# Routed experts after a convolution block: tiles in pairs, weights in the gated product, one reduction per token tile

## The chip, the core and the metric

The kernel runs on one core of a Trainium2 chip. The metric is the device time in microseconds of one execution. TensorE (PE) multiplies, VectorE (DVE), ScalarE (ACT) and GpSimd (POOL) do elementwise work, SyncE (SP) issues most loads; GpSimd also issues the indirect scatters.

## The reference, cut to what matters

```python
u = x @ W_in + b_in                       # x: 8 batches x 512 tokens x 256
x0, x1, v = split(short_conv(u), 3)
v = causal_fft_conv(v * x1, filter, filter_bias)
x = layernorm(x + (v * x0) @ W_out + b_out)
probs = softmax(x @ gate_w.T)             # 16 experts, the best 4 of each token
combine = top-4 weights, normalised
act = silu(x @ w1[e].T) * (x @ w3[e].T)   # hidden size 128, for each chosen expert e
moe = sum over e of combine[e] * (act @ w2[e].T)
shared = silu(x @ sw1.T) * (x @ sw3.T) @ sw2.T
out = layernorm(x + moe + shared)
```

## The kernel before, in words

The program has three parts, each written by hand for each engine, with semaphores between the engines.

The first is a loop over the eight batches (`batches`, with a `body` for each engine). It makes the convolution of batch i+1 and the routing of batch i-1 in one body. For each token the routing finds the four experts, their weights (`m8` times `rden`) and a row number in a DRAM table `expert_rows`, sorted by expert. ScalarE copies each token's row four times into `row` (`fill_rows`), VectorE writes the weight and the later destination into two more columns (`end_rows`), and GpSimd issues 16 indirect scatters of 128 rows per batch (`scatter`). GpSimd also adds the output bias into `xtok` (its line is 611), which VectorE needs for the residual sum `r`. The shared expert's result, with the residual, goes into DRAM as the fifth part of each token (`store_acc`).

The second part runs the expert tiles (`tiles`, with a `turn` for each engine). A tile is 128 rows of one expert; there are 160, in 20 groups of eight: groups 0 to 13 hold batches 0 to 5, groups 14 to 19 batches 6 and 7. One turn works on four tiles at different stages: it transposes tile u, makes the hidden product of tile u-2 (`AT_H`), transposes the gated product `ta` of tile u-3 (`AT_A`), and multiplies tile u-4 by w2 (`AT_Y`). Every matrix is split into a high and a low half (`xtT_hi`, `xtT_lo`, `taT_hi`, `taT_lo`), so that three matmuls make one product. SyncE loads rows into `xt`, eight buffers; a buffer is free when VectorE has copied its last two columns into `wd` (semaphore `t_wd`). ScalarE scales the result by the weight into one of four `ty` buffers, and GpSimd scatters it into `token_parts`, where each token has five parts of 256 values side by side. A `ty` buffer is free when its scatter has landed (`res_out`). At the head of each group TensorE loads the expert numbers into registers. Groups 2 to 9 also carry the last batch's 16 row scatters, two in each.

The third part (`last`) sums the parts and normalises. SyncE loads the five parts of 128 tokens into a `yb` buffer, of which there are two sets of four. VectorE adds parts 0 and 1 into `s1` (line 1454), GpSimd makes parts 2, 3 and 4 into `s2` (lines 664 and 668), VectorE adds the two (line 1465) and takes statistics (line 1149); for the last token tile VectorE also adds the fifth part itself. In names of the trace `s1` is `r` or `acc`, and the `yb` buffers are `row`, `late_parts` and `more_parts`. Batches 0 to 4 are summed between the turns of groups 15 to 19, batches 5 to 7 in a tail behind them. While tiles run, VectorE finds the root of the variance by Newton steps (`norm_part`); in the tail ScalarE's root is used.

## Time and profile before

| what | value |
| --- | --- |
| median of three runs | 682.38 us (680.13 to 684.12) |
| the profiled execution | 681.89 us, its span 680.2 us |
| mean granted TensorE clock | 0.933 |
| busy: PE, DVE, ACT, POOL | 562.6, 531.9, 400.1, 430.9 us |
| traffic | 127.69 MB by DMA, mean 188 GB/s |
| expert tiles, first transpose to last product | about 366 to 645 us |

The span goes from the first to the last instruction of the profiled execution. Busy time is the union of an engine's instructions, so two that overlap count once. No engine is busy for the whole span; which one sets the pace changes from part to part, so the page's totals have to be read by stage.

### The profile page before, as it was taken

Reading aid. Unit: us, or ns where it says so; the run is one execution under the profiler, and the core shown is the slowest. Engines: PE = TensorE matmul, PEld = TensorE weight load, DVE = VectorE, ACT = ScalarE, POOL = GpSimd, SP = SyncE. Lnnn points to the kernel's source line nnn. Section 1 sums busy time; section 2 is a strip of 40 time slices with the busy share of each in tenths; the row PEclk is TensorE's granted clock in tenths of the full one; section 3 lists DMA queues with packets and bytes.
Section 4 is the critical chain, followed back from the end, with each engine's and each line's share of the span. In section 5 each row is a group of like instructions: output and inputs, shape, how many; then the busy total and the mean of one; then the engine's idle time right before and its main releaser. Section 6 shows DMA issues by size and latency. Waiting matters only on the chain.

```text
span 680.2 us, 13537 instructions
## 1 busy us (share of the span) xinstructions
PE 562.6 (83%) x3356; PEld 491.8 (72%) x3357; DVE 531.9 (78%) x1494; ACT 400.1 (59%) x968; POOL 430.9 (63%) x414
## 2 busy tenths in 40 slices
PE   1879798999999999997877999899999996777600
PEld 0558686888878877776666999898898985767500
DVE  5247889898989999999886766665666568899877
ACT  0443454776767585663162976776777774656632
POOL 2061325277767868585637677777776678778892
PEclk9769899999999999998968999999999999888955
DMA  8329812233424243219863778766665579988674
GB/s 306 97 66 365 310 35 63 82 129 93 140 86 156 93 139 108 93 62 347 274 179 125 206 218 234 229 197 184 186 186 177 163 267 356 292 287 285 237 301 155
DMA packets 77116, 127.69 MB, mean 188 GB/s; under 512 B 10870, under 2 KB 57527, under 8 KB 76474
## 3 DMA queue, kind: packets, MB, share of 16 engines
q1 hardware_dynamic: 45548, 69.34, 33.3%
q0 software_dynamic: 22448, 49.17, 21.3%
q10 hardware_dynamic: 9086, 8.80, 3.8%
q8 instruction: 12, 0.20, 0.1%
q14 instruction: 22, 0.18, 0.1%
HBM read 81.00 MB, written 54.72 MB: 200 GB/s over the span
## 4 chain that ended last, share of the span: by engine, by line
PE 41%; DVE 31%; issue 13%; DMA 5%; POOL 5%; ACT 4%; DVEq 1%; SPq 0%; POOLq 0%; ACTq 0%
PE bank L855 6%; PE bank L857 5%; PE bank L856 5%; PE bank L686 4%; PE bank L705 4%; PE bank L894 3%; POOL expert_rows L634 3%; DMA token_parts<-ty_all,wd 3%; PE bank L728 2%; PE bank L886 2%; PE bank L795 2%; DVE prodA L1209 2%; PE bank L816 2%; DVE x1c L1130 2%; POOL token_parts L647 2%
## 5 line engine op out<-in xcount | busy, mean ns | idle before, releaser
L647 POOL DMA_INDIRECT token_parts<-ty_all,wd x160 | 157.3, 983 | 63.3 <-issue 41.9
L634 POOL DMA_INDIRECT expert_rows<-row,slot x128 | 136.1, 1063 | 90.5 <-DVE dest L1367 53.6
L855 PE MATMUL bank<-w_hi,xtT_hi 128*128 x320 | 94.1, 294 | 20.3 <-issue 13.3
L1068 ACT ACTIVATE ty_all<-bank,wd 128x256 f32<-128x256 f32 x160 | 76.8, 480 | 36.2 <-DMA token_parts<-ty_all,wd 32.3
L1413 DVE TENSOR_TENSOR ta<-bank,tsl 128x128 f32<-128x128 f32 x160 | 46.3, 289 | 60.5 <-ACT tsl L1050 57.6
L856 PE MATMUL bank<-w_lo,xtT_hi 128*128 x320 | 91.3, 285 | 0.0
L857 PE MATMUL bank<-w_hi,xtT_lo 128*128 x320 | 91.0, 285 | 0.0
L855 PEld LDWEIGHTS bank<-w_hi,xtT_hi 128*128 128x128 f32 x320 | 61.9, 194 | 24.6 <-issue 24.6
L1426 DVE TENSOR_TENSOR xtT_lo<-bank,xtT_hi 128x256 fp32r<-128x256 f32 x160 | 67.6, 422 | 1.8 <-ACT xtT_hi L1061 1.6
L1050 ACT ACTIVATE tsl<-bank 128x128 f32<-128x128 f32 x160 | 44.4, 277 | 38.2 <-PE bank L857 35.0
L1061 ACT CAST xtT_hi<-bank 128x256 fp32r<-128x256 f32 x160 | 61.9, 387 | 6.9 <-PE bank L894 6.6
L894 PE MATMUL bank<-ident,xt 128*128 128x128 f32 x320 | 62.4, 278 | 2.7 <-issue 2.0
L857 PEld LDWEIGHTS bank<-w_hi,xtT_lo 128*128 128x128 f32 x320 | 62.0, 194 | 0.0
L856 PEld LDWEIGHTS bank<-w_lo,xtT_hi 128*128 128x128 f32 x320 | 61.8, 193 | 0.0
L855 PE MATMUL bank<-w_hi,taT_hi 128*128 x160 | 59.2, 370 | 0.4 <-DVE taT_lo L1419 0.3
L686 PE MATMUL bank<-zt,mats 128*128 128x256 f32 x256 | 57.6, 381 | 1.7 <-DVE slot L1322 1.7
L886 PE MATMUL bank<-ident,ta 128*128 128x128 f32 x160 | 46.0, 287 | 15.0 <-DVE ta L1413 14.8
L795 PE MATMUL bank<-mats,Y 128*128 128x256 f32 x256 | 58.0, 386 | 0.0
L686 PEld LDWEIGHTS bank<-zt,mats 128*128 128x128 f32 x256 | 47.9, 190 | 9.0 <-DVE slot L1322 2.8
L795 PEld LDWEIGHTS bank<-mats,Y 128*128 128x128 f32 x256 | 49.2, 194 | 6.7
L1055 ACT CAST taT_hi<-bank 128x128 fp32r<-128x128 f32 x160 | 42.5, 266 | 10.7 <-PE bank L886 10.6
L950 ACT ACTIVATE up<-bank,chan 128x512 f32<-128x512 f32 x48 | 33.1, 689 | 26.7 <-PE bank L705 26.5
(174 smaller groups left out, 1497.4 us busy)
## 6 DMA issues: line engine op xcount, KB each, us to landing
xt<-expert_rows SPq DMA_DIRECT2D x160, 129.0 KB
row<-token_parts SPq DMA_DIRECT2D x12, 640.0 KB, 5.2
more_parts<-token_parts SPq DMA_DIRECT2D x12, 640.0 KB, 8.1
late_parts<-token_parts SPq DMA_DIRECT2D x8, 640.0 KB, 7.4
expert_rows<-in_c_pad SPq DMA_DIRECT2D x2, 2064.0 KB, 13.2
expert_rows<-in_c_pad SPq DMA_DIRECT2D x32, 129.0 KB
xT_hi<-in_xT POOLq DMA_DIRECT2D x8, 512.0 KB, 4.5
xT<-in_xT SPq DMA_DIRECT2D x8, 512.0 KB, 3.8
```

The source lines that it names most:

```text
L634: pool.indirect_dma_start(out=rows_d, out_offset=bass.IndirectOffsetOnAxis(ap=slot[q][:, n:n + 1], axis=0), in_=row[:, n // TOPK, n % TOPK ...
L647: pool.indirect_dma_start(out=parts_d, out_offset=bass.IndirectOffsetOnAxis(ap=wd[:, v, 1:2].bitcast(U32), axis=0), in_=ty[v % 4], in_offs ...
L686: mm = te_.matmul(ps[:, part * D:(part + 1) * D], fwd[:, 2 * s + t, part * NF * P + f * P:part * NF * P + (f + 1) * P], src[:, 2 * s + t, ...
L795: mm = te_.matmul(bank[4 + c][:, s * 2 * P:(s + 1) * 2 * P], Y[:, f, s, part * D + c * P:part * D + (c + 1) * P], inv[:, part * NF + f, s ...
L855: te_.matmul(ps, x_hi, w_hi, start=first, stop=False)
L856: te_.matmul(ps, x_hi, w_lo, start=False, stop=False)
L857: return te_.matmul(ps, x_lo, w_hi, start=False, stop=last)
L886: te_.transpose(bank[4 + v % 2][:, 0:P], ta[:, v % 2, :], ident[:, :]).then_inc(t_aT, 1)
L894: mm = te_.transpose(bank[v % 2][:, c * P:(c + 1) * P], xt[:, v, c * P:(c + 1) * P], ident[:, :])
L1061: sc.copy(xtT_hi[:, v % 2, :, :].rearrange("p c t -> p (c t)"), bank[v % 2][:, 0:D]).then_inc(t_xhi, 1)
L1068: sc.activation(ty[v % 4], bank[6 + v % 2][:, 0:D], ACT.Identity, scale=wd[:, v, 0:1]).then_inc(t_yc, 1)
L1426: ve.tensor_tensor(xtT_lo[:, v % 2, :, :].rearrange("p c t -> p (c t)"), bank[v % 2][:, 0:D], xtT_hi[:, v % 2, :, :].rearrange("p c t -> p ...
```

## The change

Tiles go in pairs. A turn now transposes pair j, makes the hidden products of pair j-1, the w2 products of pair j-3 and the transposes of pair j-2; each bank holds both tiles of a pair, so each instruction of ScalarE and VectorE is twice as wide. The weight is multiplied in with the gated product, on VectorE, one instruction for each tile, and ScalarE's last step is a plain copy. `wd` is gone: weight and destination are read from `xt`, which has 16 buffers (`RING`) and is free when the tile's result has landed. `ty` has eight buffers. Loops are unrolled over two groups.

In the sums, one VectorE reduction over the five parts takes the place of two adds on VectorE and two on GpSimd, and `yb` has one set of four buffers, so a load waits for the statistics of the same token tile one batch before. In the batch loop GpSimd adds the bias for the next batch ahead of the scatters, and ScalarE fills all rows of the batch before the last in the last body instead of half of them one body earlier. SyncE's first row load waits for the last residual sum (`dve_r`) instead of the last forward transform.

```diff
-AT_H, AT_A, AT_Y = 2, 3, 4
+AT_H, AT_A, AT_Y = 1, 2, 3
+PAIRS = UNROLL // 2
+RING = 2 * UNROLL
...
-        yb = [[tokens_parts(place, t) for t in range(TT - 1)] + [tokens_parts(late_parts, q)]
-              for q, place in enumerate((early, more_parts[:, :]))]
+        yb = [early[:, t * PARTS * D:(t + 1) * PARTS * D] for t in range(TT - 1)] + [more_parts]
...
@@ SyncE
-                after(sp, t_wd, (g - 1) * UNROLL + u + 1)
-                sp.dma_start(xt[:, u, :], rows_d[bass.ds(first_row[u], P), :]).then_inc(ld_xt[u], 16)
+                for u in (2 * j, 2 * j + 1):
+
+                    after(sp, res_out[u], 16 * (g - 1))
+                    sp.dma_start(xt[:, q * UNROLL + u, :], rows_d[bass.ds(first_row[u], P), :]).then_inc(ld_xt[q * UNROLL + u], 16)
...
-                    sp.wait_ge(ln_bn, TT * (B + b - 2) + t + 1)
-                    sp.dma_start(yb[q][t],
+                    if not is0(b):
+                        sp.wait_ge(ln_bn, TT * (B + b - 1) + t + 1)
+                    sp.dma_start(yb[t],
...
@@ GpSimd
-                    pool.indirect_dma_start(
-                        out=parts_d, out_offset=bass.IndirectOffsetOnAxis(ap=wd[:, v, 1:2].bitcast(U32), axis=0),
-                        in_=ty[v % 4], in_offset=None
-                    ).then_inc(res_out[v % 4], 16)
+                    for u in (2 * v, 2 * v + 1):
+                        pool.indirect_dma_start(
+                            out=parts_d,
+                            out_offset=bass.IndirectOffsetOnAxis(ap=xt[:, q_ * UNROLL + u, D + 1:D + 2].bitcast(U32), axis=0),
+                            in_=ty[:, u, :], in_offset=None
+                        ).then_inc(res_out[u], 16)
...
@@ ScalarE
                 if not has_this(i):
-                    fill_rows(i - 2, q, range(TT // 2, TT))
+                    fill_rows(i - 2, q)
...
-                    if is_end(i):
-                        fill_rows(i - 1, 1 - q, range(0, TT // 2))
...
-                    after(act, res_out[v % 4], 16 * uses4(gv, v))
-                    sc.activation(ty[v % 4], bank[6 + v % 2][:, 0:D], ACT.Identity,
-                                  scale=wd[:, v, 0:1]).then_inc(t_yc, 1)
+                    for u in (2 * v, 2 * v + 1):
+                        after(act, res_out[u], 16 * g_)
+                    sc.copy(ty[:, 2 * v:2 * v + 2, :].rearrange("p a d -> p (a d)"), bank[6 + v % 2][:, :]).then_inc(t_yc, 1)
...
@@ VectorE
-                    ve.tensor_tensor(ta[:, v % 2, :], bank[2 + v % 2][:, HID:2 * HID], tsl[:, v % 2, :], ALU.mult
-                                     ).then_inc(t_a, 1)
+                    for a in range(2):
+                        ve.scalar_tensor_tensor(ta[:, v % 2, a, :], bank[2 + v % 2][:, (2 * a + 1) * HID:(2 * a + 2) * HID],
+                                                xt[:, q_ * UNROLL + 2 * v + a, D:D + 1], tsl[:, v % 2, a, :],
+                                                ALU.mult, ALU.mult).then_inc(t_a, 1)
...
-                    ve.tensor_tensor(s1[q][:, t, :], yb[q][t][:, 0:D], yb[q][t][:, D:2 * D], ALU.add).then_inc(f_sum, 1)
...
-                    ve.tensor_tensor(s1[q][:, t, :], s1[q][:, t, :], s2[:, t, :], ALU.add).then_inc(f_s1, 1)
+                    ve.tensor_reduce(out=s1[q][:, t, :], in_=yb[t].rearrange("p (k d) -> p d k", k=PARTS), axis=AXX, op=ALU.add
+                                     ).then_inc(f_s1, 1)
```

VectorE in group 15, two turns of the kernel before with the work on one token tile; line 1413 makes `ta`, 1419 `taT_lo`, 1426 `xtT_lo`, and 1465 adds GpSimd's `s`:

```order
L1454 TENSOR_TENSOR r<-row 128x256
L1465 TENSOR_TENSOR r<-r,s 128x256
L1149 BN_STATS stats<-r 128x6
L1413 TENSOR_TENSOR ta<-bank,tsl 128x128
L1419 TENSOR_TENSOR taT_lo<-bank,taT_hi 128x128
L1426 TENSOR_TENSOR xtT_lo<-bank,xtT_hi 128x256
L1430 COPY wd<-xt 128x2
```

The same place after the change, one turn with a pair of tiles:

```order
L1397 TENSOR_TENSOR xtT_lo<-bank,xtT_hi 128x512
L1406 SCALAR_TENSOR_TENSOR ta<-bank,xt,tsl 128x128 x2
L1414 TENSOR_TENSOR taT_lo<-bank,taT_hi 128x256
L1440 TENSOR_REDUCE r<-row 128x256
L1132 BN_STATS stats<-r 128x6
```

Before, the four tile instructions stand twice for each token tile; now three kinds stand once, wider, and one reduction replaces both adds.

ScalarE in the last two bodies of the batch loop of the kernel before, where 1038 fills `row`, 1024 is the shared expert's silu (`aT`), 971 stores `acc`, and 1014 copies `x1T` for the last batch's routing:

```order
L1019 ACTIVATE ex<-lg 128x64
L1038 COPY row<-x_0 128x4x256 x2
L1024 ACT_TABLE_LOAD
L1024 ACTIVATE aT<-bank 128x512
L1032 ACT_TABLE_LOAD
L1032 ACTIVATE sd<-var 128x4
L1001 ACTIVATE x_1<-r,nmr,rstd 128x256 x4
L971 DMA token_parts<-acc 128x4x256
L1038 COPY row<-x_0 128x4x256 x2
L1014 COPY x1T<-bank 128x512 x2
```

And after the change:

```order
L1001 ACTIVATE ex<-lg 128x64
L1004 ACT_TABLE_LOAD
L1004 ACTIVATE aT<-bank 128x512
L1012 ACT_TABLE_LOAD
L1012 ACTIVATE sd<-var 128x4
L983 ACTIVATE x_1<-r,nmr,rstd 128x256 x4
L953 DMA token_parts<-acc 128x4x256
L1018 COPY row<-x_0 128x4x256 x4
L996 COPY x1T<-bank 128x512 x2
```

Two of the four row copies have moved from ahead of silu to ahead of the copy of `x1T`.

GpSimd in the same bodies of the kernel before, where 611 adds the bias, 589 and 591 finish `x0`, and 634 scatters a batch's rows:

```order
L634 DMA expert_rows<-row,slot 73728x258 x16
L611 TENSOR_TENSOR xtok<-xtok,bout 128x1024
L589 TENSOR_TENSOR x_1<-x_1,prodA 128x512
L591 TENSOR_TENSOR x_1<-x_1,up 128x512
L589 TENSOR_TENSOR x_1<-x_1,prodA 128x512
L591 TENSOR_TENSOR x_1<-x_1,up 128x512
L634 DMA expert_rows<-row,slot 73728x258 x16
L611 TENSOR_TENSOR xtok<-xtok,bout 128x1024
```

And after the change:

```order
L620 DMA expert_rows<-row,slot 73728x258 x16
L578 TENSOR_TENSOR x_1<-x_1,prodA 128x512
L580 TENSOR_TENSOR x_1<-x_1,up 128x512
L578 TENSOR_TENSOR x_1<-x_1,prodA 128x512
L580 TENSOR_TENSOR x_1<-x_1,up 128x512
L569 TENSOR_TENSOR xtok<-xtok,bout 128x1024
L620 DMA expert_rows<-row,slot 73728x258 x32
```

The bias add, which stood behind each batch's scatters, now stands ahead of the next batch's.

## Rows read from the trace of the kernel before

**Rows 1.** Stage windows: us, then each engine's busy time and instructions, clock, DMA.

```profile
0.00:366.00 366.00, 320.02 (x1436) 260.00 (x1438) 305.64 (x625) 197.44 (x290) 202.73 (x169) 0.94 0.48 152
366.00:552.20 186.20, 173.18 (x1421) 168.17 (x1422) 117.28 (x492) 135.99 (x475) 133.28 (x139) 0.99 0.65 194
552.20:645.00 92.80, 69.30 (x502) 63.59 (x499) 82.30 (x304) 56.94 (x184) 74.56 (x83) 0.94 0.88 302
```

**Rows 2.** VectorE's busy time in one group of eight tiles.

```profile
571.40:590.15 18.75, 16.93 (x63) 0.91 0.91 297
```

**Rows 3.** Windows in the second stage, all engines, PE first.

```profile
450.00:500.00 50.00, 45.99 (x377) 44.09 (x377) 31.27 (x127) 34.77 (x128) 37.68 (x39) 1.00 0.63 186
500.00:548.00 48.00, 44.59 (x376) 43.77 (x375) 29.62 (x127) 36.49 (x126) 31.26 (x33) 1.00 0.55 167
```

**Rows 4.** Timeline of VectorE, one tile of that group: start, us, instruction.

```profile
578.11 0.27 DVE L1413 TENSOR_TENSOR ta<-bank,tsl 128x128 f32<-128x128 f32 x1
578.30 0.28 DVE L1419 TENSOR_TENSOR taT_lo<-bank,taT_hi 128x128 fp32r<-128x128 f32 x1
578.49 0.41 DVE L1426 TENSOR_TENSOR xtT_lo<-bank,xtT_hi 128x256 fp32r<-128x256 f32 x1
578.83 0.16 DVE L1430 COPY wd<-xt 128x2 int32<-128x2 int32 x1
578.89 0.15 DVE L1486 SCALAR_TENSOR_TENSOR root<-rstd 128x4 f32<-128x4 f32 x1
```

**Rows 5.** Groups of VectorE's instructions, 571.4 to 608.4.

```profile
L1465 DVE TENSOR_TENSOR r<-r,s 128x256 f32<-128x256 f32 x4 | 3.9, 966 | 0.0
```

**Rows 6.** Timeline of VectorE in the tail.

```profile
644.92 0.42 DVE L1454 TENSOR_TENSOR acc<-more_parts 128x256 f32<-128x256 f32 x1
...
667.58 0.17 DVE L1156 TENSOR_TENSOR mdiff<-stats 128x4 f32<-128x4 f32 x1
...
669.48 0.76 DVE L1454 TENSOR_TENSOR acc<-more_parts 128x256 f32<-128x256 f32 x2
...
674.10 0.43 DVE L1149 BATCH_NORM_STATS2 stats<-acc 128x6 f32<-128x256 f32 x1
```

**Rows 7.** VectorE's reductions (ns min/median/max), and two adds in a row.

```profile
L1279 DVE TENSOR_REDUCE maskp<-onehot x8: 582/592/606, 121.6 to 358.2; 128x64 f32<-128x256 f32 x8
...
L1319 DVE TENSOR_REDUCE slot_f<-onehot x8: 419/420/420, 129.3 to 365.4; 128x16 f32<-128x256 f32 x8
...
L1268 DVE TENSOR_REDUCE den<-m x8: 170/170/171, 120.3 to 356.9; 128x4 f32<-128x16 f32 x8
...
236.39 1.29 DVE L1301 TENSOR_TENSOR acc<-bank,x 128x512 f32<-128x512 f32 x2
```

**Rows 8.** Timeline at the end of the batches.

```profile
333.99 3.60 PE L816 MATMUL bank<-x1T,sw 128*128 128x512 f32 x8
...
337.20 1.99 ACT L1038 COPY row<-x 128x1024 f32<-128x1024 f32 x2 [5.78 <-DMA expert_rows<-row,slot]
...
340.50 0.60 ACT L1024 ACTIVATE aT<-bank 128x512 f32<-128x512 f32 x1
...
349.81 1.07 ACT L1014 COPY x1T<-bank 128x512 f32<-128x512 f32 x2 [0.86 <-PE bank L784]
```

**Rows 9.** Waits from 366 to 552.2: us in total, times, longest.

```profile
ACT ty_all L1068 <- DMA token_parts<-ty_all,wd: 23.2, 29, 2.1
...
PEld bank L855 <- issue: 15.3, 16, 1.4
```

**Rows 10.** The page's costliest groups: busy us, mean ns, idle before.

```profile
L647 POOL DMA_INDIRECT token_parts<-ty_all,wd x160 | 157.3, 983 | 63.3 <-issue 41.9
```

**Rows 11.** Timeline at the start of group 15, three engines.

```profile
548.90 0.34 SPq L556 DMA_DIRECT2D row<-token_parts  x1
...
552.15 0.38 PE L894 MATMUL bank<-ident,xt 128*128 128x128 f32 x2
...
553.39 0.42 DVE L1454 TENSOR_TENSOR r<-row 128x256 f32<-128x256 f32 x1
```

More of the change, by code:

```diff
@@ L582, in rest_x, with add_bias @@
                                         op=ALU.subtract).then_inc(pool_xlo, 1)
+            def add_bias(i):
+                pool.wait_ge(ld_xtok, 16 * (i + 1))
+                nc.gpsimd.tensor_tensor(out=xtok[:, :, :], in0=xtok[:, :, :],
+                                        in1=bout[:, :].unsqueeze(1).broadcast_to([P, TT, D]),
+                                        op=ALU.add).then_inc(pool_xb, 1)
             def conv_x0(i, q):
@@ L599, in _ @@
             pool.wait_ge(ld_out, 32)
+            add_bias(0)
             def body(i, q, h):
@@ L619, in body @@
                     rest_x(i + 2)
+                if has_next(i):
+                    add_bias(i + 1)
                 if not is0(i):
@@ new lines, in turn @@
+                pair = back(g, j, q, h, 0)
+                if pair:
+                    for a in range(2):
+                        at = q * UNROLL + 2 * j + a
+                        pe_e.wait_ge(ld_xt[at], 16 * (h + 1))
+                        for c in range(DC):
+                            mm = te_.transpose(bank[j % 2][:, (a * DC + c) * P:(a * DC + c + 1) * P], xt[:, at, c * P:(c + 1) * P],
+                                               ident[:, :])
+                    mm.then_inc(t_xT, 1)
@@ new lines, in turn @@
+                pair = back(g, j, q, h, AT_H)
+                if pair:
+                    _, v, _, _, k = pair
+                    pe_e.wait_ge(t_xlo, k + 1)
+                    for a in range(2):
+                        e = expert[2 * (j - AT_H + AT_Y) + a]
+                        for c in range(DC):
+                            at = bass.ds(e * (DC * 2 * HID) + c * 2 * HID, 2 * HID)
+                            mm = products((w13_hi[:, at], w13_lo[:, at]),
+                                          (xtT_hi[:, v % 2, a, c, :], xtT_lo[:, v % 2, a, c, :]),
+                                          bank[2 + v % 2][:, a * 2 * HID:(a + 1) * 2 * HID], c == 0, c == DC - 1)
+                    mm.then_inc(t_h, 1)
@@ L900, in turn @@
+                pair = back(g, j, q, h, AT_Y)
+                if pair:
+                    _, v, _, _, k = pair
                     if isinstance(k, int) and k == 0:
                         pe_e.wait_ge(dve_slot, SLOT_N * B)
-                    e = expert[u]
                     pe_e.wait_ge(t_alo, k + 1)
-                    at = bass.ds(e * D, D)
-                    products((w2_hi[:, at], w2_lo[:, at]), (taT_hi[:, v % 2, :], taT_lo[:, v % 2, :]),
-                             bank[6 + v % 2][:, 0:D], True, True).then_inc(t_y, 1)
+                    for a in range(2):
+                        at = bass.ds(expert[2 * j + a] * D, D)
+                        mm = products((w2_hi[:, at], w2_lo[:, at]), (taT_hi[:, v % 2, a, :], taT_lo[:, v % 2, a, :]),
+                                      bank[6 + v % 2][:, a * D:(a + 1) * D], True, True)
+                    mm.then_inc(t_y, 1)
@@ L908, in second_table @@
+                pair = back(g, j, q, h, AT_A)
+                if pair:
+                    _, v, _, _, k = pair
+                    pe_e.wait_ge(t_a, 2 * (k + 1))
+                    for a in range(2):
+                        mm = te_.transpose(bank[4 + v % 2][:, a * P:(a + 1) * P], ta[:, v % 2, a, :], ident[:, :])
+                    mm.then_inc(t_aT, 1)
             def second_table(g):
@@ new lines, in turn @@
+                pair = back(g, j, q, h, 0)
+                if pair:
+                    _, v, _, _, k = pair
+                    dve.wait_ge(t_xhi, k + 1)
+                    ve.tensor_tensor(xtT_lo[:, v % 2, :, :, :].rearrange("p a c t -> p (a c t)"), bank[v % 2][:, :],
+                                     xtT_hi[:, v % 2, :, :, :].rearrange("p a c t -> p (a c t)").bitcast(F32), ALU.subtract
+                                     ).then_inc(t_xlo, 1)
+                pair = back(g, j, q, h, AT_H)
```

279 lines of the change are left out of this document (104 added, 175 removed).

## The prediction

> **What bounds the kernel now.** I read the stage windows first [rows 1]: for 366 us the eight batches go through convolution and routing, for 186.2 us TensorE runs expert tiles of batches 0 to 5 at a clock of 0.99, for 92.8 us (552.2 to 645) it runs the tiles of batches 6 and 7 while VectorE sums finished tokens, and the last 35.2 us have almost no matmul. TensorE is busy 173 of 186 us in the second stage and 69 of 93 in the third; there VectorE has 82 of 93.
>
> Next the third stage by group of eight tiles. From 571.4 to 590.15 VectorE is busy 16.93 of 18.75 us [rows 2], while TensorE needs some 12.3 us for such a group (500 to 548 us: 376 matmuls in 48 us, 12 to a tile, is 31.3 tiles, 12.26 us for eight [rows 3]). The timeline of VectorE shows how it spends them [rows 4]: from start to start, ta costs 0.19 us, taT_lo 0.19, xtT_lo 0.34, the copy wd 0.06, so 0.8 us a tile. An add of s2 into s1 takes 0.966 us in the mean [rows 5], where one of the same width with nothing beside it takes 0.42 [rows 11]: GpSimd is adding into s2 at the same time. So this stage is VectorE's, and it will be so after the change.
>
> The tail, last [rows 6]: VectorE begins batch 5 at 644.92 and ends the last statistics at 674.53, four token tiles of three batches in 29.6 us, of which 1.9 us each for two norms (667.58 to 669.48). Then 5.6 us to the end.
>
> **The price on which all hangs: the new sum.** It reads five rows of 256 values, 1,280 elements, each next element 1 KB on, and stands 32 times on VectorE's path (20 beside the tiles, 12 in the tail). The trace has no such instruction. Its reductions [rows 7]: slot_f reads 256 elements that lie in a row in 0.420 us, den 16 elements as four runs of four in 0.170; that is 0.250 / 240 = 1.04 ns an element on 0.153 us. maskp reads 256 elements as four at a stride of 64 bytes for each output and takes 0.592. den has short runs too and pays nothing for them, so I put maskp's surplus on the stride: (0.592 - 0.153) / 256 = 1.715 ns an element. Bounds for the sum: 0.153 + 1,280 x 1.04 ns = 1.49 us if the stride costs nothing, 0.153 + 1,280 x 1.715 ns = 2.35 us at maskp's rate. I take 2.35, the row with the nearest pattern; maskp's surplus put on its 64 outputs instead (2.7 ns each, of which the sum has 256) would give 1.49 + 0.69 = 2.2. Above 2.35 the trace has no bound.
>
> The trace shows the strided reduction dearer. The Trainium skill (SBUF — State Buffer, the note on 16-byte "cachelines") says that accesses which each cross to a new line pay a penalty; by that rule the sum is at the strided price. The skill (VectorE: DVE Perf Modes, perf-mode tier table) gives tensor_reduce one element a cycle whatever the type; by that alone it would be at the low price; the same page advises restructuring where this op is on a hot path. By the first rule the span is the 693.7 worked out below, by the second the 666 of the first rival.
>
> **The change part by part**, against the profiled span of 680.2.
>
> 1. *Batches 0 to 6.* add_bias stands ahead of the 16 scatters instead of behind them, so it no longer runs on GpSimd beside VectorE's onehot, which can only help. But TensorE is nearly full in this stage, 320 of 366 us with the start included: I allow -1 us (0 to -2). The new add waits for xtok, loaded after the residual; the scatters that stand behind it start later than that load lands, so nothing is charged.
>
> 2. *The last batch.* Now ScalarE's two row copies wait 5.78 us for batch 5's scatters, and silu, queued behind them, starts at 340.50 [rows 8]. Moved behind silu, they free it: the products that it needs start at 333.99 and last 3.60 us [rows 8], so silu can start near 337.7, -2.8 us. Given back: four copies of 1 us instead of two stand ahead of x1T, which runs at 349.81 [rows 8]. They wait for batch 6's accumulator (346.9 now, 344.1 then) and end at 348.1, and x1T starts there. Net -1.7 us (0 to -3).
>
> 3. *Groups 0 to 14.* Matmuls, transposes and the indirect DMAs on POOL are the same in number. VectorE and ScalarE get fewer, wider instructions, but TensorE waits little for them: hidden, worth nothing. The four ty buffers make ScalarE wait 23.2 us in 29 waits [rows 9]: a scatter takes POOL 0.98 us and 0.3 of issue [rows 10], 1.27 from start to start, so eight and two late ones 12.7 us in groups 2 to 9, against TensorE's 12.26. Eight buffers and the 16-tile ring let TensorE run ahead of it: 450 to 500 us has 31.4 tiles in 50, against 31.3 in 48 later [rows 3], 0.5 us a group over some five groups, -2.4 us (0 to -5). Loads of 14 expert numbers for 12 and half the loop branches I put at nothing together.
>
> 4. *Hand-over at group 15.* SyncE may load tokens of batch 0 when group 13's results have landed. It did so at 548.90 [rows 11], 3.3 us ahead of group 15's first transpose (552.15). Now the last pair of group 13 is transposed 16 us ahead of group 15 (five turns of 2.8 us, two group changes of 1 us [rows 9]), and its results have landed 17.2 us after that: three turns and a change 9.5, to the last product 2.5, the copy 0.8, two scatters 2.3, the landing 2.1. So the load goes out 1.3 us behind that transpose. Its data take up to 4.5 us (548.90 to the first add at 553.39 [rows 11]), and the first sum starts 5.8 us behind the transpose instead of 1.2: +4.6 us (2 to 6). The xt loads queued behind them on SyncE come as late; that is the same stall.
>
> 5. *Groups 15 to 19.* VectorE a group: four pairs at 0.61 (512 wide: two acc in 1.29, one 0.68 [rows 7]) + 2 x 0.22 + 0.33 = 1.38 each, 5.5; four sums with statistics at 2.35 + 0.38 = 2.73, 10.9; norm steps without GpSimd's adds beside them 2.7; waits 0.2: 19.3 us, and 16.7 in the first, which has no norm. 16.7 + 4 x 19.3 = 93.9 against 644.92 - 553.39 = 91.5: +2.4. The same count for the kernel before (8 x 0.8, eight adds 3.1, statistics 1.4, norm 2.7) gives 13.6 of the measured 18.3; the 4.7 left are collisions with GpSimd's adds and waits. So 0.9 of tile work, 3.1 of adds and nearly all of the 4.7 go, and four sums of 2.35, 9.4 us, come. The drain is by pairs: +2.0 us.
>
> 6. *Tail.* Batch 5: 10.9 + 2.7 = 13.6; batches 6 and 7: 1.9 + 10.9 each. Together 39.2 against 29.6: +9.6. GpSimd used to make two of the four adds in parallel; nothing does now. One set of yb buffers instead of two costs nothing here: a slot is free after its sum, and loads of 640 KB take 5 to 8 us against 10.9.
>
> Sum: -1 - 1.7 - 2.4 + 4.6 + 2.4 + 2.0 + 9.6 = +13.5. Span 693.7; the profiled execution was 1.7 us over its span (681.89 against 680.2) and 0.5 under the median, so some 695.4 and 695.9. I say **695**. With d the price of one sum, the span moves by 32 d: break-even is 2.35 - 13.5 / 32 = 1.93 us.
>
> **The rivals.**
>
> *Free stride: faster.* If the sum reads an element a cycle, 1.49 us, then 32 x 0.86 = 27.5 us come off the span: 666.2, a time of 668. (That is how it comes out by the perf-mode tier table of the Trainium skill, VectorE: DVE Perf Modes.) For it speak slot_f and den; against it maskp, the only strided reduction [rows 7]. The place is VectorE from group 15 to the end, and it decides below 1.93 us. TensorE's 12.3 us a group still fits under VectorE's 15.9. Chance 0.22.
>
> *A dearer stride.* All five rows lie a kilobyte apart, maskp's only 64 bytes. At 2.8 us it is 710, and each further 0.1 us adds 3.2. Nothing in the trace shows it or excludes it. Chance 0.13.
>
> *The ring starves TensorE.* xt was free after its transposes, at t_wd; now it is free when the result of the tile has landed, since the scatter reads its index there. By the count of part 4 that is 17.2 us after the transposes, of the ring's 24.5; 7.3 us remain for the load, less whatever POOL lags in groups 2 to 9. If TensorE then goes at POOL's 12.7 us with 0.3 more for the load, part 3 turns from -2.4 into +5: 702. For it speaks that POOL is nearly full there; against it that four ty buffers held TensorE closer to POOL before. Chance 0.10.
>
> **How the numbers follow.** Forecast (690 to 700) 0.50, free stride 0.22, dearer 0.13, ring 0.10; 0.05 for gains in the early parts that cancel the tail (near 682). A measurement of this kernel can hardly tell less than 0.5%, 3.4 us, from no change. Faster: 0.22 and a little of the rest, 0.25; same 0.06; slower 0.69. The three slower cases hold 0.73, so eight in ten must reach the free stride: 668 to 711. The likeliest case's own range is 689 to 701 (2.2 to 2.5 us a sum, and the bounds of parts 1 to 4).
>
> **What would show it.** The reduction near 2.35 us, flat, no longer stretched by GpSimd; groups 15 to 19 near 19 us with TensorE waiting for ta; silu of the last batch some 3 us earlier; first sum 5 to 6 us after group 15's first transpose; three batches in the tail in 39 us. The forecast falls if the reduction is under 1.9 us, or if transposes wait for xt in groups 2 to 14.

## The result, and the profile after

| | before | after |
|---|---|---|
| time, median | 682.65 us (4 runs, 680.13 to 684.12) | 699.65 us (4 runs, 698.52 to 702.02) |
| ratio | | 1.0254, 95% interval 1.0225 to 1.0282 |
| profiled execution: span, clock | 680.2 us, 0.933 | 698.7 us, 0.924 |
| VectorE busy | 531.9 us (78%) in 1,494 instructions | 540.4 us (77%) in 1,141 instructions |

The change made the kernel slower by 2.5%, 17 us. The forecast was 695 us with a range of 668 to 711.

The stage windows of the changed kernel (core 0; us, then each engine's busy time and instructions, clock, DMA) answer to [rows 1]:

```profile
0.00:366.00 366.00, 318.38 (x1444) 259.03 (x1445) 302.06 (x625) 197.87 (x292) 203.79 (x171) 0.94 0.49 155
366.00:552.20 186.20, 170.74 (x1422) 166.66 (x1422) 105.62 (x256) 107.81 (x242) 130.76 (x135) 0.99 0.61 187
552.20:645.00 92.80, 63.42 (x443) 58.23 (x444) 87.04 (x182) 39.79 (x89) 36.79 (x38) 0.92 0.83 273
```

In the first two stages TensorE's time and clock hardly differ. In the third VectorE has 87.0 of 92.8 us where it had 82.3, with 182 instructions for 304, and TensorE gets 443 matmuls done where it did 502; GpSimd's busy time halves (74.6 to 36.8), mostly since its adds are gone. The price on which the forecast hung stands in VectorE's groups from 553 us to the end:

```profile
L1440 DVE TENSOR_REDUCE r<-row 128x256 f32<-128x1280 f32 x12 | 28.7, 2389 | 1.5 <-DMA row<-token_parts 1.5
L1440 DVE TENSOR_REDUCE acc<-row 128x256 f32<-128x1280 f32 x12 | 28.4, 2369 | 0.0
L1397 DVE TENSOR_TENSOR xtT_lo<-bank,xtT_hi 128x512 fp32r<-128x512 f32 x19 | 13.0, 683 | 0.2
L1406 DVE SCALAR_TENSOR_TENSOR ta<-bank,xt,tsl 128x128 f32<-128x128 f32 x40 | 12.0, 342 | 1.3 <-ACT tsl L1037 1.3
```

By the trace's groups a sum takes 2.37 to 2.40 us in the mean (2.29 to 2.36 alone in the tail, up to 2.46 beside tiles), against the 2.35 of the forecast. VectorE's timeline shows one block of a group, pair and sum and statistics, and the next sum:

```profile
604.40 2.44 DVE L1440 TENSOR_REDUCE r<-row 128x256 f32<-128x1280 f32 x1
606.88 0.43 DVE L1132 BATCH_NORM_STATS2 stats<-r 128x6 f32<-128x256 f32 x1
607.22 0.67 DVE L1397 TENSOR_TENSOR xtT_lo<-bank,xtT_hi 128x512 fp32r<-128x512 f32 x1
607.82 0.60 DVE L1406 SCALAR_TENSOR_TENSOR ta<-bank,xt,tsl 128x128 f32<-128x128 f32 x2
608.33 0.41 DVE L1414 TENSOR_TENSOR taT_lo<-bank,taT_hi 128x256 fp32r<-128x256 f32 x1
608.66 2.46 DVE L1440 TENSOR_REDUCE r<-more_parts 128x256 f32<-128x1280 f32 x1
```

4.26 us from sum to sum: 2.82 for the sum with its statistics, 1.44 for the pair. Of two tiles the pair replaces 1.6 us [rows 4], so the wider instructions do save something, 0.16 us a pair; the sum costs many times that. The chain of waits of that stage shows who stands behind it (552.2 to 645; us in total, times, longest):

```profile
PE bank L831 <- DVE xtT_lo L1397: 23.5, 15, 3.1
...
PEld bank L853 <- DMA xt<-expert_rows: 3.7, 2, 3.2
```

TensorE waits 23.5 us for the xtT_lo that is queued behind a sum, where the forecast had it wait for ta. At the hand-over, the rows that answer to [rows 11], from three engines' timelines:

```profile
548.25 0.65 PE L853 MATMUL bank<-ident,xt 128*128 128x128 f32 x4 [0.71 <-issue]
...
549.73 0.34 SPq L538 DMA_DIRECT2D row<-token_parts  x1
550.27 0.85 SPq L511 DMA_DIRECT2D xt<-expert_rows  x2
...
553.87 2.37 DVE L1440 TENSOR_REDUCE r<-row 128x256 f32<-128x1280 f32 x1 [1.47 <-DMA row<-token_parts]
...
554.22 0.44 PE L853 MATMUL bank<-ident,xt 128*128 128x128 f32 x2 [2.96 <-DMA xt<-expert_rows]
```

Group 15 begins 3.9 us earlier (552.15 before), the load of batch 0 goes out 1.5 us behind its first transpose and the first sum starts 5.6 us behind it, where it was 1.24. So at the first sum the two kernels are level again: 553.87 and 553.39. TensorE meanwhile waits 2.96 us for the second pair's rows. The tail, to be read beside [rows 6]:

```profile
655.61 2.36 DVE L1440 TENSOR_REDUCE acc<-row 128x256 f32<-128x1280 f32 x1
...
670.01 2.34 DVE L1440 TENSOR_REDUCE r<-row 128x256 f32<-128x1280 f32 x1
...
682.22 2.34 DVE L1440 TENSOR_REDUCE acc<-row 128x256 f32<-128x1280 f32 x1
...
692.61 0.43 DVE L1132 BATCH_NORM_STATS2 stats<-acc 128x6 f32<-128x256 f32 x1
```

From batch 0's first sum to batch 5's it is 101.7 us (91.5 before), from there to the last statistics 37.4 (29.6), and 5.7 to the end as before. 0.5 + 10.2 + 7.8 = 18.5 us, the difference of the spans: all of it lies behind the first sum.

### The profile page after: what moved, and what is told of

It is laid out like the page before. It is cut to its first block, busy times and chain, and to the rows that moved or that the text cites. A ratio compares the mean times of both kernels' runs of the same rounds, so it can differ in the third digit from the quotient of the medians.

```text
span 698.7 us, 12093 instructions
## 1 busy us (share of the span) xinstructions
PE 560.6 (80%) x3356; PEld 491.0 (70%) x3357; DVE 540.4 (77%) x1141; ACT 359.0 (51%) x648; POOL 379.1 (54%) x351
## 4 chain that ended last, share of the span: by engine, by line
PE 56%; DVE 29%; issue 8%; DMA 3%; ACT 3%; POOL 1%; SPq 0%; DVEq 0%; ACTq 0%; POOLq 0%
PE bank L681 7%; PE bank L771 6%; PE bank L831 6%; PE bank L832 6%; PE bank L833 6%; DVE acc L1440 5%; PE bank L662 5%; DVE r L1440 5%; PE bank L704 4%; PE bank L792 4%; PE bank L853 4%; PE bank L785 2%; PE bank L887 2%; DVE ta L1406 1%; DVE stats L1132 1%
## 5 line engine op out<-in xcount | busy, mean ns | idle before, releaser
L634 POOL DMA_INDIRECT token_parts<-ty,xt x160 | 155.0, 969 | 113.1 <-ACT ty L1046 73.0
L1037 ACT ACTIVATE tsl<-bank 128x256 f32<-128x256 f32 x80 | 30.9, 386 | 82.3 <-PE bank L833 82.3
L1397 DVE TENSOR_TENSOR xtT_lo<-bank,xtT_hi 128x512 fp32r<-128x512 f32 x80 | 55.1, 689 | 20.5 <-ACT xtT_hi L1031 17.7
L1406 DVE SCALAR_TENSOR_TENSOR ta<-bank,xt,tsl 128x128 f32<-128x128 f32 x160 | 48.6, 345 | 28.3 <-ACT tsl L1037 28.3
L1046 ACT COPY ty<-bank 128x512 f32<-128x512 f32 x80 | 47.0, 587 | 35.5 <-PE bank L833 35.0
L1414 DVE TENSOR_TENSOR taT_lo<-bank,taT_hi 128x256 fp32r<-128x256 f32 x80 | 33.8, 422 | 37.7 <-ACT taT_hi L1052 37.5
L1031 ACT CAST xtT_hi<-bank 128x512 fp32r<-128x512 f32 x80 | 47.6, 597 | 26.3 <-PE bank L853 26.3
L853 PEld LDWEIGHTS bank<-ident,xt 128*128 128x128 f32 x320 | 37.6, 145 | 28.4 <-issue 22.2
L831 PE MATMUL bank<-w_hi,taT_hi 128*128 x160 | 46.6, 291 | 3.6 <-DVE taT_lo L1414 3.6
L681 PE MATMUL bank<-xT_hi,w_in_hi 128*128 128x512 f32 x96 | 40.1, 418 | 8.2 <-DVE w_in_lo L1161 8.2
```

What stands on the lines that cost most here:

```text
L634: pool.indirect_dma_start(out=parts_d, out_offset=bass.IndirectOffsetOnAxis(ap=xt[:, q_ * UNROLL + u, D + 1:D + 2].bitcast(U32), axis=0), ...
L681: mm = te_.matmul(bank[n % 2][:, :], w[:, c, m * P:(m + 1) * P], x[:, c, :], start=(c == 0 and part == 0), stop=(c == DC - 1 and part == 2))
L831: te_.matmul(ps, x_hi, w_hi, start=first, stop=False)
L853: mm = te_.transpose(bank[j % 2][:, (a * DC + c) * P:(a * DC + c + 1) * P], xt[:, at, c * P:(c + 1) * P], ident[:, :])
L1397: ve.tensor_tensor(xtT_lo[:, v % 2, :, :, :].rearrange("p a c t -> p (a c t)"), bank[v % 2][:, :], xtT_hi[:, v % 2, :, :, :].rearrange("p ...
L1406: ve.scalar_tensor_tensor(ta[:, v % 2, a, :], bank[2 + v % 2][:, (2 * a + 1) * HID:(2 * a + 2) * HID], xt[:, q_ * UNROLL + 2 * v + a, D:D ...
```

## The experiments

Each time is a median with its ratio to the kernel before on the same chip. The changed kernel has 1.0254 on that scale; 0.1 points of it (0.001) are 0.68 us. Differences in us below are taken from these ratios, those between stretches of a kernel from one profile of each.

**1. The stride taken away.** Same count, width and output, but the five elements of a sum lie side by side. The kernel leaves the reference's sum out: it adds the wrong five values.

```diff
-ve.tensor_reduce(out=s1[q][:, t, :], in_=yb[t].rearrange("p (k d) -> p d k", k=PARTS), axis=AXX, op=ALU.add)
+ve.tensor_reduce(out=s1[q][:, t, :], in_=yb[t].rearrange("p (d k) -> p d k", k=PARTS), axis=AXX, op=ALU.add)
```

> The changed kernel, with the 32 reductions reading their 1,280 elements in the order in which they lie, five neighbours to an output, so that it leaves the reference's sum out (it adds the wrong five values); count, width and output are the same. Theory, the stride is what costs: a reduction takes 1.49 us (slot_f's rate, 1.04 ns an element on 0.153 us) in place of the 2.41 measured, and the time falls by 32 x 0.9 = 29 us to about 671. Rival, the reduction costs 1.7 to 1.8 ns an element however it reads: no change, 700. Between them (part of the price on the stride, part on the 256 outputs): 1.49 + 0.69 = 2.2 us and 693.

Measured: 673.78 us, ratio 0.986 (0.9831 to 0.9888). Its row in VectorE's groups:

```profile
L1440 DVE TENSOR_REDUCE acc<-row 128x256 f32<-128x1280 f32 x12 | 17.8, 1481 | 0.0
```

1.48 us, the lower bound of the forecast, where the same instruction with the stride takes 2.37: the stride is the whole surplus, and nothing of it lies on the 256 outputs. The 26.9 us that come off the ratio are 0.84 for each of the 32 sums, of the 0.89 by which each got shorter. With the free read the kernel is faster than the one before, by 1.4%.

**2. Where the stride begins to cost.** The first three token tiles of a batch read at 8, 16 and 64 bytes; in these the kernel leaves the reference's sum out.

```diff
+s = (2, 4, 16)[t]
+ve.tensor_reduce(out=s1[q][:, t, :].rearrange("p (x s) -> p x s", s=s),
+                 in_=yb[t].rearrange("p (x k s) -> p x s k", k=PARTS, s=s), axis=AXX, op=ALU.add)
```

> The changed kernel, with the reductions of the first three token tiles of each batch reading the five elements of an output 8, 16 and 64 bytes apart instead of 1,024 (the fourth tile as it is), so that it leaves the reference's sum out in these tiles. Element by element in a row is 1.48 us, a kilobyte apart 2.3 to 2.4. Theory, each element that does not lie next to the one before costs the full price: 2.3 us for all four, time 699. Rival one, the price is for each element that lies 16 bytes or more on: 8 bytes about 1.9, 16 and 64 bytes and 1 KB 2.3. Rival two, it grows with the distance: 1.6, 1.8, 2.0, 2.35.

Measured: 696.04 us, one execution, so the rows of its trace are what counts. VectorE's timeline in the tail, one batch, tiles in the order 8, 16, 64 and 1,024 bytes:

```profile
667.13 1.48 DVE L1442 TENSOR_REDUCE r<-row 128x256 f32<-128x1280 f32 x1
668.99 2.41 DVE L1442 TENSOR_REDUCE r<-row 128x256 f32<-128x1280 f32 x1
671.77 2.29 DVE L1442 TENSOR_REDUCE r<-row 128x256 f32<-128x1280 f32 x1
674.45 2.29 DVE L1446 TENSOR_REDUCE r<-more_parts 128x256 f32<-128x1280 f32 x1
```

A step, not a slope: 8 bytes cost nothing, 16 bytes cost as much as a kilobyte. That decides between the rivals, though both had put 8 bytes too high (1.9 and 1.6; the theory that every gap costs is out). The Trainium skill (SBUF — State Buffer, the note on 16-byte "cachelines") says that accesses which each cross to a new line pay; these rows agree, in the place of the step too. It also settles what the forecast called the dearer stride: between 16 bytes and 1 KB more distance costs nothing more.

**3. The sum as three adds on VectorE.**

```diff
-ve.tensor_reduce(out=s1[q][:, t, :], in_=yb[t].rearrange("p (k d) -> p d k", k=PARTS), axis=AXX, op=ALU.add)
+ve.tensor_tensor(yb[t][:, 0:2 * D], yb[t][:, 0:2 * D], yb[t][:, 2 * D:4 * D], ALU.add).then_inc(f_sum, 1)
+dve.wait_ge(f_sum, 2 * (b * TT + t) + 1)
+ve.tensor_tensor(s1[q][:, t, :], yb[t][:, 0:D], yb[t][:, D:2 * D], ALU.add).then_inc(f_sum, 1)
+dve.wait_ge(f_sum, 2 * (b * TT + t) + 2)
+ve.tensor_tensor(s1[q][:, t, :], s1[q][:, t, :], yb[t][:, TOPK * D:], ALU.add).then_inc(f_s1, 1)
```

> The changed kernel, with each reduction replaced by three VectorE adds: parts 0 and 1 plus parts 2 and 3 in one add of 512, then the two halves, then the fifth part. From rows: a 512-wide add is 0.60 us from start to start, two of 256 at 0.42 each and waits of some 0.1 between, so 1.6 to 1.75 us against 2.41. Theory, VectorE is the bound from group 15 to the end and all of it lies on its path: 32 x 0.7 = 22 us less, 677 (674 to 681). Rival, the wait of TensorE's chain behind each block is what counts in groups 15 to 19, and only the 12 sums of the tail pay back: 12 x 0.7, 691.

Measured: 675.66 us, ratio 0.9877 (0.9849 to 0.9905), faster than both kernels. One tile in its tail, from VectorE's timeline:

```profile
651.37 0.69 DVE L1440 TENSOR_TENSOR row<-row 128x512 f32<-128x512 f32 x1
652.10 0.42 DVE L1442 TENSOR_TENSOR r<-row 128x256 f32<-128x256 f32 x1
652.56 0.43 DVE L1444 TENSOR_TENSOR r<-r,row 128x256 f32<-128x256 f32 x1
653.02 0.43 DVE L1132 BATCH_NORM_STATS2 stats<-r 128x6 f32<-128x256 f32 x1
```

1.65 us for the sum, with the waits for each result in it. It is under the forecast's break-even of 1.93, and the time lands on the faster side. The difference to the changed kernel, 3.77 points or 25.7 us, is 0.80 us for each of 32 sums that got 0.74 shorter: all 32 stand on the path, the 20 beside the tiles too.

**4. The sum shared with GpSimd as before, all else changed.**

```diff
+# GpSimd, for each token tile
+nc.gpsimd.tensor_tensor(out=yb[t][:, 2 * D:3 * D], in0=yb[t][:, 2 * D:3 * D], in1=yb[t][:, 3 * D:4 * D], op=ALU.add)
+nc.gpsimd.tensor_tensor(out=yb[t][:, 2 * D:3 * D], in0=yb[t][:, 2 * D:3 * D], in1=yb[t][:, TOPK * D:], op=ALU.add)
 # VectorE
+ve.tensor_tensor(s1[q][:, t, :], yb[t][:, 0:D], yb[t][:, D:2 * D], ALU.add)
+ve.tensor_tensor(s1[q][:, t, :], s1[q][:, t, :], yb[t][:, 2 * D:3 * D], ALU.add)
```

> The changed kernel, with the sum as the kernel before makes it: GpSimd adds parts 2, 3 and 4 (in place), VectorE adds the first two and then GpSimd's result. Pairs, ring, orders and the hand-over stay. Theory, the sum is all that made the change slower: the tail goes back from 37.4 to 29.6 us, groups 15 to 19 from 20.3 us each to some 17.7 (18.3 before, less 0.6 of narrower tile work), so 7.8 + 13 us less: 679 (675 to 683). Rival, the pairs (wide copies held up by GpSimd, the drain by pairs, the late hand-over) cost as well: it stays over 686.

Measured: 680.9 us, ratio 0.9952 (0.9928 to 0.9976). This lies in the theory's 675 to 683. The rest of the change, without its sum, is a small gain of 0.5%. Batch 0's first sum to batch 5's takes 88.4 us (91.5 before), the tail 32.3 (29.6 before), in which VectorE waits 2.1 us for tokens and once for GpSimd:

```profile
DVE acc L1468 <- POOL row L661: 4.0, 1, 4.0
```

**5. The new sum alone, in the kernel before.** GpSimd's adds and VectorE's two are replaced by the reduction; nothing else changes.

```diff
-nc.gpsimd.tensor_tensor(out=s2[:, t, :], ...)   # both
-ve.tensor_tensor(s1[q][:, t, :], ...)           # both
+ve.tensor_reduce(out=s1[q][:, t, :], in_=yb[q][t].rearrange("p (k d) -> p d k", k=PARTS), axis=AXX, op=ALU.add)
```

> The kernel before, with only the sum changed: one reduction of 5 x 256 on VectorE for each token tile, no adds on GpSimd; tiles one by one, four result buffers, two sets of token rows, old orders. Theory, the sum carries the slowdown: groups 15 to 19 at 8 x 0.8 + 4 x 2.8 + 2.9 = 20.5 us against 18.3, so about +10, and +7.8 in the tail: 698 to 702, as slow as the whole change. Rival, half of the slowdown is the late hand-over and the pairs: 690 or less.

Measured: 701.74 us, ratio 1.026 (1.0227 to 1.0293): the sum alone costs as much as the whole change, as the theory had it. 102.8 us to batch 5's first sum and 37.5 for the tail, where the changed kernel has 101.7 and 37.4.

**6. The two moved steps put back.**

```diff
+if is_end(i):
+    fill_rows(i - 1, 1 - q, range(0, TT // 2))   # ScalarE, ahead of the silu
-fill_rows(i - 2, q)
+fill_rows(i - 2, q, range(TT // 2, TT))
...
-if has_next(i):
-    add_bias(i + 1)                              # GpSimd, ahead of the scatters
```

> The changed kernel, with the two moved steps of the batches put back where they stood before: ScalarE copies half of batch 6's rows ahead of the last silu and half behind, GpSimd's add_bias of a batch stands behind the scatters of the batch before. Theory, these two moves give the 3.9 us by which the changed kernel reaches group 15 earlier, for the most part: the last silu goes back from 336.6 to 340.5 us, the first expert transpose comes 3 us later, and so does everything behind it: about 702.5 (701 to 704). Rival, the start of group 15 is set by the expert groups' own pace and half of this is caught up: 700 to 701.

Measured: 703.41 us, ratio 1.0289 (1.0252 to 1.0326), 2.4 us over the changed kernel with intervals that overlap; the profile is clearer. The last silu goes back from 336.58 to 340.16, the first expert transpose from 364.75 to 367.03, the first transpose of group 15 from 548.25 to 552.36. The nine other profiles of kernels with the moved steps and eight result tiles have the last of these between 546.1 and 549.0, so the theory holds as far as one profile tells: the moves are what lets group 15 start earlier. The collision with add_bias, which one of them was to take away, is gone only in part. VectorE's groups in the batches of this kernel have:

```profile
L1256 DVE TENSOR_TENSOR onehot<-eidx,i 128x256 f32<-128x256 f32 x8 | 11.4, 1430 | 0.0
```

and those of the changed one:

```profile
L1256 DVE TENSOR_TENSOR onehot<-eidx,i 128x256 f32<-128x256 f32 x8 | 5.4, 673 | 0.0
```

Out from under add_bias the first onehot falls to 0.67 us in the mean. But in two of the eight batches add_bias now runs beside the second one (line 1299), as the timelines of GpSimd and VectorE in the changed kernel show:

```profile
127.42 2.35 POOL L569 TENSOR_TENSOR xtok<-xtok,bout 128x1024 f32<-128x1024 f32 x1 [12.32 <-DMA xtok<-in_x]
127.69 2.36 DVE L1299 TENSOR_TENSOR onehot<-onehot,slot_e 128x256 f32<-128x256 f32 x1
...
305.49 2.35 POOL L569 TENSOR_TENSOR xtok<-xtok,bout 128x1024 f32<-128x1024 f32 x1 [4.30 <-DMA xtok<-in_x]
305.87 2.25 DVE L1299 TENSOR_TENSOR onehot<-onehot,slot_e 128x256 f32<-128x256 f32 x1
```

The other six take 0.42 us. Both long ones end 0.28 us behind the end of GpSimd's add, the one that began 0.27 us after it as well as the one that began 0.38 us after it: what the collision costs is the rest of GpSimd's instruction. So the collision has moved, and part of it is gone: over the eight batches both onehots together take 12.5 us in the changed kernel, 14.7 here.

**7. Four result tiles for eight.**

```diff
-after(act, res_out[u], 16 * g_)
-sc.copy(ty[:, 2 * v:2 * v + 2, :] ...)
+after(act, res_out[u + 4], 16 * g_)  or, in pairs 2 and 3,  act.wait_ge(res_out[u - 4], 16 * (g_ + 1))
+sc.copy(ty[:, 2 * (v % 2):2 * (v % 2) + 2, :] ...)
```

> The changed kernel with four result tiles ty in place of eight (each used again by the pair two later), ring of 16 row tiles unchanged. Theory, four result tiles held TensorE to GpSimd's pace in groups 2 to 9 before: ScalarE waits 20 us or more for them again (0.5 us now), group 15 starts 1 to 2.5 us later and the time is 701 to 702. Rival, TensorE's own pace of 12.2 to 12.4 us a group sets it and the wait of ScalarE stays beside it: no change, 700.

Measured: 708.17 us, ratio 1.0362 (1.0324 to 1.04), 7.4 us over the changed kernel. The waits from 366 to 552 us:

```profile
ACT ty L1049 <- DMA token_parts<-ty,xt: 30.6, 25, 2.2
...
POOL token_parts L634 <- ACT ty L1049: 17.5, 11, 4.2
```

In the changed kernel the first of these is 0.5 us. The first expert transpose to group 15's takes 190.8 us in place of 183.5: the whole difference. The theory's wait is there, and its cost three to seven times the 1 to 2.5 us that it gave. A pair's copy waits for both of its tiles, and GpSimd then waits for the copy, so with four tiles, as I read these rows, the wait goes round between the two instead of being taken up. With four tiles this stretch is 4.7 us longer than in the kernel before, with eight 2.6 us shorter: pairs need the eight.

**8. Rows first in group 15.** SyncE asks for all row tiles of the group ahead of the token loads.

```diff
+whole = isinstance(g, int) and g == NTURN0 + 1
-for u in (2 * j, 2 * j + 1):
+for u in (range(UNROLL if j == 0 else 0) if whole else (2 * j, 2 * j + 1)):
```

> The changed kernel, with only SyncE's order in group 15 changed: the row tiles of all four pairs are asked for first, then the four loads of batch 0's finished tokens (before, the first of these stands ahead of pairs 1 to 3 and waits for all results of group 13). Theory, the first VectorE block of group 15 takes 19.9 us instead of the 16.7 of the forecast since TensorE waits 2.96 us for rows that stand behind the token load: this wait goes, the second sum starts 2 to 3 us earlier, time 697 to 698. Rival, pairs 2 and 3 wait for group 13's last results as well, and the token loads come as much later as the rows come earlier: no change or up to 1 us more, 700.

Measured: 700.12 us, ratio 1.0236 (1.0206 to 1.0266): no difference to be told. VectorE's timeline at its first two sums:

```profile
555.04 2.31 DVE L1441 TENSOR_REDUCE r<-row 128x256 f32<-128x1280 f32 x1 [3.10 <-DMA row<-token_parts]
...
559.17 2.40 DVE L1441 TENSOR_REDUCE r<-row 128x256 f32<-128x1280 f32 x1
```

TensorE's wait is gone and the second sum follows the first by 4.1 us (6.4 in the changed kernel), but the first is 1.2 us later behind the rows, and batch 1's first sum comes at 573.33 instead of 573.74. One load or the other is late.

**9. Both together, and the tail's adds interleaved.** Experiments 3 and 8 in one kernel; then the same with the adds of two token tiles taking turns in batches 5 to 7 (512-wide adds of both, then the halves of both, then the fifth parts, then the statistics).

```diff
+for t in ts:                     # two token tiles
+    ve.tensor_tensor(yb[t][:, 0:2 * D], yb[t][:, 0:2 * D], yb[t][:, 2 * D:4 * D], ALU.add)
+for t in ts:
+    ve.tensor_tensor(s1[q][:, t, :], yb[t][:, 0:D], yb[t][:, D:2 * D], ALU.add)
+for t in ts:
+    ve.tensor_tensor(s1[q][:, t, :], s1[q][:, t, :], yb[t][:, TOPK * D:], ALU.add)
```

> The three VectorE adds of the earlier run and SyncE's rows-first order in group 15 together. Theory, they add up: the adds gave 24 us, the order alone some 0.5 us; with the cheaper sum VectorE is less behind in group 15, so the rows that come earlier may give up to 2 us: 673 to 676. Rival, the later token load (1.2 us later in the earlier run) is now on the path: 677.

> As the run with both, and in the tail (batches 5 to 7) the three adds and the statistics of two token tiles take turns, so that no add stands right behind the one whose result it reads. In the run with three adds the starts of a tile's instructions in the tail were 0.72, 0.46, 0.46 and 0.35 us apart, 1.99 a tile. Theory, 0.12 us of each of the three is the wait for a result: 12 x 0.3 = 3.6 us less than the run with both, 671 to 672. Rival, the loads of tokens (2.6 MB a batch) bound the tail at 9 us a batch: 1 us less or nothing.

Measured: 675.66 us, ratio 0.9887 (0.9847 to 0.9927), and 675.95 us, ratio 0.9907 (0.9873 to 0.9941). The order of loads adds nothing to the three adds. Interleaved, a batch's second pair of tiles reads in VectorE's timeline:

```profile
653.90 0.69 DVE L1443 TENSOR_TENSOR row<-row 128x512 f32<-128x512 f32 x1 [0.31 <-DMA row<-token_parts]
655.56 0.69 DVE L1443 TENSOR_TENSOR more_parts<-more_parts 128x512 f32<-128x512 f32 x1 [0.97 <-DMA more_parts<-token_parts]
656.17 0.42 DVE L1447 TENSOR_TENSOR r<-row 128x256 f32<-128x256 f32 x1
656.50 0.42 DVE L1447 TENSOR_TENSOR r<-more_parts 128x256 f32<-128x256 f32 x1
656.84 0.42 DVE L1450 TENSOR_TENSOR r<-r,row 128x256 f32<-128x256 f32 x1
```

The rival held: VectorE's own work shrinks, and it now waits 3.9 us for token loads in the tail, where the run before it waited for none; their tails take 29.0 and 28.9 us from batch 5's first sum to the last statistics. So the next bound is the loads of 2.6 MB a batch into one set of buffers. The forecast's "costs nothing here" for the single set held with the slow sums and with three adds in order, and failed here. The interleaved order also frees the buffers of two tiles together instead of one by one, so a part of the waits may be its own; two sets of buffers with the cheap sum were not tried.

**10. One add back on GpSimd.** GpSimd adds the fifth part into the fourth, VectorE makes a 512-wide and a 256-wide add.

```diff
+# GpSimd, in a block behind the two scatters
+nc.gpsimd.tensor_tensor(out=yb[t][:, 3 * D:4 * D], in0=yb[t][:, 3 * D:4 * D], in1=yb[t][:, TOPK * D:], op=ALU.add)
+# VectorE
+ve.tensor_tensor(yb[t][:, 0:2 * D], yb[t][:, 0:2 * D], yb[t][:, 2 * D:4 * D], ALU.add)
+ve.tensor_tensor(s1[q][:, t, :], yb[t][:, 0:D], yb[t][:, D:2 * D], ALU.add)
```

> As the run with both, but GpSimd adds the fifth part into the fourth (one add for each token tile, in place), and VectorE makes two adds, 512 and 256 wide. Theory, GpSimd's add takes 1 us and holds VectorE's instructions beside it up by about what VectorE saves (an add took 0.97 us beside it in the kernel before and 0.42 alone): within 3 us of the run with both, 672 to 678. Rival, it saves 0.45 us for each tile with no collision: 32 x 0.45 = 14 us, 661.

Measured: 709.15 us, ratio 1.0354 (1.0303 to 1.0405). Neither had it: some 32 us slower than the three adds. The waits from 553 us on:

```profile
POOL token_parts L636 <- ACT ty L1055: 49.4, 12, 5.8
...
DVE row L1450 <- POOL row L653: 36.1, 12, 5.2
PE bank L840 <- DVE xtT_lo L1406: 34.5, 10, 4.7
```

A ring of four engines, each in its own order. GpSimd's add stands behind two scatters that wait for ty; ty waits for TensorE; TensorE waits for xtT_lo; and xtT_lo is queued behind the sum that waits for GpSimd's add. The split of experiment 4 escapes it, as I read it because there VectorE takes GpSimd's result up a block later than it is made.

**11. The same, with GpSimd's add ahead of the scatters.**

```diff
+last(*b, 2 * j)         # the add
+last(*b, 2 * j + 1)
 turn(g, j, q, h)        # two scatters
-last(*b, 2 * j)
-last(*b, 2 * j + 1)
```

> The run with one GpSimd add, with only GpSimd's order changed: in each block the add stands ahead of the two scatters instead of behind them. Theory, in that run four engines went in lockstep (GpSimd's add stood behind scatters that wait for ty, VectorE's sum waited for that add for 36 us in 12 waits, TensorE waited 34.5 us for the xtT_lo queued behind the sum): with the add ahead these waits go and it comes within 5 us of the three VectorE adds, 670 to 681. Within that, 0.46 us a tile saved against GpSimd's 0.77 us add beside VectorE decides; I put it at 673. Rival, GpSimd's queue still carries the wait (the add of a block stands behind the scatters of the block before): over 690.

Measured: 684.9 us, ratio 1.0019 (0.9996 to 1.0042), between the two. The waits from 553 us on:

```profile
POOL row L656 <- DMA row<-token_parts: 20.7, 7, 6.0
POOL token_parts L639 <- ACT ty L1058: 17.8, 6, 3.7
...
DVE row L1453 <- POOL row L656: 11.5, 3, 5.3
```

VectorE's wait falls from 36 to 11.5 us. What is left is the same ring with a load in it: an add waits up to 6 us for its tokens and the scatters stand behind it. That the order of one queue is worth some 23 us is shown; why it stays 9 us over the three adds is argued from these rows only.

## Why the prediction was right, and where it was off

The mechanism was the forecast one: the strided read makes the sum 2.35 us, VectorE is the bound from group 15 to the end, and all 32 sums stand on its path. Experiments 1, 3 and 5 show each part: without the stride 26.9 us go, with three adds 25.7 go, and the sum alone in the old kernel brings 17.8. The price was no luck: it was taken from a reduction at a stride of 64 bytes, and experiment 2 shows 64 bytes and a kilobyte to cost the same. The free-stride rival, forecast at 668, came out at 673.8 when its condition was made true, too low by about as much as the forecast itself. One sign was wrong: TensorE waits for xtT_lo, not for ta; both are VectorE's.

By its parts, against a forecast span of 693.7 and a measured one of 698.7:

- *Batches and last batch (-1 and -1.7):* the last silu started 3.9 us earlier and x1T 3.0, forecast -3.8 and -2.7. But only 1.3 of it reached the first expert transpose (364.75 against 366.02), 1.4 less than the forecast. The chain through that place shows where it went: the products behind x1T took 6.29 us in place of 5.06, and the step ahead of the first transpose 1.85 in place of 1.36. The step goes with the pairs: 1.85 or 1.86 us in every kernel that has them, 1.37 in that of experiment 5. The products lie in a stretch in which the clock is granted at 0.50, the 1.2 GHz level, and comes back to 1.00 at about 357.5 us before and 356.9 after. Starting 3.0 us earlier, they spend more of themselves in it; their two windows (shown behind this list) have a mean clock of 0.71 before and 0.57 after. Length times clock is 3.59 us in both, as in experiments 5 (6.48 at 0.55, 3.56) and 6 (5.13 at 0.70, 3.59), and 3.60 is what eight such products take at 1.00 [rows 8]. So 1.2 us of the earlier start go to the clock. When the clock falls and comes back here is not explained.
- *Groups 0 to 14 (-2.4):* 366.02 to 552.15 was 186.1 us, 364.75 to 548.25 is 183.5: -2.6. The wait for ty fell from 23.2 us [rows 9] to 0.5. Experiment 7 shows the buffers behind it; in pairs they are worth 7.4 us, so what the eight buffers did here was in the main to avoid a loss that pairs would have brought. The -2.6 isn't theirs alone: in experiment 6, which keeps them, this stretch takes 185.3 us, where all other kernels with pairs and eight buffers have 182.5 to 183.6, and in the kernel of experiment 5, with the old four, it takes 187.7. How the 3.9 us at group 15 divide between the moved steps and the buffers is not settled.
- *Hand-over (+4.6):* +4.4. Load at +1.5 and first sum at +5.6 us, forecast +1.3 and +5.8.
- *Groups 15 to 19 and the drain (+2.4 and +2.0):* **this term was mis-sized.** It was to be 93.9 + 2.0 = 95.9 us and is 101.7, 5.8 more. Two parts: the first group takes 19.87 us for 16.7. Of that 2.0 are VectorE's waits behind the late rows at the hand-over (the forecast had called that "the same stall", but it comes once more, on TensorE's side), and 0.7 the six small instructions with which batch 0's norm begins (573.01 to 573.74), where the forecast had no norm at all. And each full group takes 20.0 for 19.3: 1.45 a pair for 1.38, 2.80 a sum with statistics for 2.73, 2.9 of norm steps for 2.7. Experiment 8 shows that the waits of the first part aren't removed by this reordering.
- *Tail (+9.6):* +7.8. The sums are nearly as forecast (2.68 with statistics for 2.73), the norms between batches take 1.4 us instead of 1.9. The half microsecond is one small instruction beside a GpSimd add in the kernel before, 0.71 us where it takes 0.16 alone:

```profile
667.63 0.72 POOL L664 TENSOR_TENSOR s<-late_parts 128x256 f32<-128x256 f32 x1
667.66 0.71 DVE L1157 TENSOR_TENSOR msum<-stats 128x4 f32<-128x4 f32 x1
```

The windows of the products behind x1T, before and after (us, then each engine's busy time and instructions, clock, DMA):

```profile
354.53:359.59 5.06, 5.04 (x9) 1.90 (x8) 4.15 (x20) 1.54 (x2) 4.15 (x4) 0.71 0.46 159
351.54:357.83 6.29, 6.27 (x8) 2.34 (x8) 3.72 (x19) 1.54 (x2) 5.07 (x5) 0.57 0.94 271
```

The misses, part by part, are 1.4 - 0.2 - 0.2 + 5.8 - 1.8 = 5.0 us, the whole of the difference. That the tail errs the other way is luck: without it the forecast would have been 6.8 us too low.

The rivals: a dearer stride is excluded (no more for 1 KB than for 64 bytes). The ring did not starve TensorE in groups 2 to 14: its waits for xt come to 2.4 us at most there, all near 436 us, and the groups got faster. By the letter the forecast had named such a wait as a sign against itself.

What stayed open in the forecast was whether the rest of the change is worth anything. Experiment 4 gives it: 0.5% faster. In its profile group 15 starts 3.2 us earlier than before, the hand-over turns that into 1.2 us later at the first sum, the stretch to batch 5's first sum gives 3.1 us, and the tail costs 2.7. With the sum as three adds it is 1.2% faster, which is the version to keep.

## What to carry to other kernels

One instruction for several is not one price: look at how far apart its elements lie. Here a reduction over an axis whose elements are 16 bytes or more apart cost 1.6 times the one that reads in order, and three plain adds beat it. Before moving work off an engine that collides with another, count whether the receiver is the bound of the stage; here VectorE was, 32 times. And before moving work onto a queue in program order, follow what stands ahead of it: one add on GpSimd, placed behind two scatters, closed a ring of waits through four engines and cost some 32 us.
